# Later batches take the output slices in the order 3, 4, 1, 2, GpSimd casts part 1 of the weights, and ring loads stand two steps behind the stores

## What is computed

```python
masked_w = weight * mask[None, :, :]              # (8, 512, 512)
w_bot = jnp.einsum('bg,got->bot', y, masked_w)    # one 512x512 matrix for each of 128 batches
x = x + jnp.einsum('bnt,bot->bno', x, w_bot) + bias
```

## Time and profile before

| | us |
|---|---|
| median of three runs | 644.95 |
| lowest and highest of them | 641.86, 645.34 |
| the profiled execution, its own time | 650.79 |
| its span, first to last instruction | 649.0 |
| TensorE busy | 625.6 |
| ScalarE busy | 304.4 |
| VectorE busy | 306.9 |
| GpSimd busy | 109.0 |

### The profile page before, as it was taken

The page is one execution under the profiler, slowest core; times in us unless marked ns, Lnnn a source line. Parts: engine busy times, 40 slices in busy tenths (PEclk is TensorE's granted clock), DMA queues, the critical chain, the costliest instruction groups (busy, mean ns, idle before and its releaser), DMA issues.

```text
span 649.0 us, 18471 instructions
## 1 busy us (share of the span) xinstructions
PE 625.6 (96%) x7911; PEld 597.0 (92%) x7911; DVE 306.9 (47%) x328; ACT 304.4 (47%) x529; POOL 109.0 (17%) x92
## 2 busy tenths in 40 slices
PE   8999996979999978999999999999999999999997
PEld 3467996979999978999999999999999999999997
DVE  5996663758643432444343443434343443434221
ACT  0131673757755433554545544554545444554500
POOL 5796653566500000000000000000000000000000
PEclk9999997989999997999999999999999999999999
DMA  8999989998999995665789996665789997663112
GB/s 323 419 325 314 302 273 305 278 282 277 294 364 287 318 315 173 179 178 150 201 235 346 299 305 195 180 179 156 180 252 339 276 315 210 179 179 116 50 66 82
DMA packets 52400, 157.28 MB, mean 242 GB/s; under 512 B 7696, under 2 KB 20096, under 8 KB 40576
## 3 DMA queue, kind: packets, MB, share of 16 engines
q1 hardware_dynamic: 33200, 121.92, 62.3%
q10 hardware_dynamic: 19120, 34.19, 16.6%
HBM read 109.94 MB, written 46.14 MB: 240 GB/s over the span
## 4 chain that ended last, share of the span: by engine, by line
PE 86%; DMA 6%; DVE 4%; issue 2%; ACT 1%; POOL 1%; ACTq 0%; DVEq 0%
PE ps L584 66%; PE ps L565 15%; PE ps L544 5%; DMA xs<-in_x 4%; DVE raw L468 1%; DMA w_parts<-parts 1%; DVE wbot L481 1%; ACT wbot L423 1%; DVE ring L473 1%; DMA ring<-in_first 1%; POOL raw L382 1%; DVE staged L494 0%; POOL parts L384 0%; ACT parts L418 0%; ACT parts L414 0%
## 5 line engine op out<-in xcount | busy, mean ns | idle before, releaser
L584 PE MATMUL ps<-wbot,xs 128*128 128x128 f32 x4096 | 482.5, 278 | 6.9 <-DMA xs<-in_x 6.1
L584 PEld LDWEIGHTS ps<-wbot,xs 128*128 128x128 f32 x4096 | 469.8, 194 | 10.6 <-DMA xs<-in_x 6.5
L423 ACT ACTIVATE wbot<-ps 128x512 f32<-128x512 f32 x464 | 267.6, 611 | 238.8 <-PE ps L584 128.4
L494 DVE TENSOR_TENSOR staged<-ps,bias_sb 128x512 f32<-128x512 f32 x128 | 88.5, 691 | 310.1 <-PE ps L584 309.8
L473 DVE COPY ring<-ring 32x4096 bf16<-32x4096 bf16 x116 | 142.7, 1231 | 10.6 <-DMA ring<-w_parts 7.2
L565 PE MATMUL ps<-yv,ring 112*128 112x64 bf16 x3712 | 122.2, 193 | 11.3 <-ACT wbot L423 10.9
L565 PEld LDWEIGHTS ps<-yv,ring 112*128 112x128 bf16 x3712 | 119.3, 98 | 13.3 <-ACT wbot L423 12.4
L382 POOL TENSOR_TENSOR raw<-raw,parts 128x512 f32<-128x512 f32 x32 | 45.8, 1430 | 55.3 <-ACT parts L414 55.2
L468 DVE TENSOR_TENSOR raw<-raw,mask_sb 128x512 f32<-128x512 f32 x32 | 43.0, 1351 | 7.5 <-DMA raw<-in_w 7.0
L384 POOL TENSOR_TENSOR parts<-raw 128x512 bf16<-128x512 f32 x32 | 42.2, 1319 | 2.5
L414 ACT ACTIVATE parts<-raw 128x512 bf16<-128x512 f32 x32 | 20.0, 626 | 45.6 <-DVE raw L468 30.1
(11 more groups left out here) (13 smaller groups left out, 6.5 us busy)
## 6 DMA issues: line engine op xcount, KB each, us to landing
ring<-w_parts SPq DMA_DIRECT2D x232, 256.0 KB, 6.2
xs<-in_x SPq DMA_DIRECT2D x32, 1024.0 KB, 14.4
out<-staged ACTq DMA_DIRECT2D x128, 256.0 KB, 3.8
w_parts<-parts SPq DMA_DIRECT2D x32, 384.0 KB, 10.7
raw<-in_w SPq DMA_DIRECT2D x16, 512.0 KB, 11.3
mask_sb<-in_mask SPq DMA_DIRECT2D x8, 256.0 KB, 10.3
xs<-in_w SPq DMA_DIRECT2D x1, 1024.0 KB, 9.0
ring<-in_w SPq DMA_DIRECT2D x2, 512.0 KB, 16.6
```

Source lines behind the costliest of these rows:

```text
L423: eng.activation(chunk_place(b, k), chunk_sums(b, k), ACT.Copy).then_inc(s_ev_a, 1)
L494: eng.tensor_tensor(staged[:, n % OUTB, :].rearrange("p (b o) -> p b o", b=GB), ps2[n % S2B][:, :].rearrange("p (b o) -> p b o", b=GB), bi ...
L584: ins = eng.matmul(ps2[n % S2B][:, b * SL:(b + 1) * SL], xs[:, load % GROUPS * GB + b, k, :], at, start=(k == 0), stop=(k == KT - 1))
```

## The change

- Units 4 to 15 take the slices in the order 3, 4, 1, 2 (`slice_of`) instead of 1, 2, 3, 4; the host puts the output together accordingly. Units 4 and 5 so read parts that units 2 and 3 have read before, and the halves of tiles 20 to 31 are first used by units 6 and 7 (bursts 48 to 59). `fresh` and `tiles_of` follow.
- `TILES_AT` is written out. Tiles up to 19 keep their steps; 20 to 25 go to steps 15, 17, 18, 20, 21 and 23, and 26 to 31 to steps 35, 36, 37, 38, 40 and 41. Stores and raw loads follow by their rules.
- From step 5 on (`BY_POOL`) GpSimd casts part 1 in front of its two subtractions, and holds the wait for the store of tile t - 5. ScalarE keeps part 2.
- `kept` counts tiles stored two steps ago instead of one, so fresh ring loads stand a step later in SP's queue: bursts 20 to 22 in step 9 (8 before), 24 to 26 in 13 (12), 28 to 30 in 17 (16).

```diff
@@ -51,10 +51,9 @@
 
 
 EARLY = 4
-TILES_AT = {0: (4, 5)}
-for _t in range(EARLY + 2, TILES):
-    _n = 1 + (_t - EARLY - 2) * 15 // 16
-    TILES_AT[_n] = TILES_AT.get(_n, ()) + (_t,)
+TILES_AT = {0: (4, 5), 1: (6, 7), **{_t - 6: (_t,) for _t in range(8, 20)},
+            15: (20,), 17: (21,), 18: (22,), 20: (23,), 21: (24,), 23: (25,),
+            35: (26,), 36: (27,), 37: (28,), 38: (29,), 40: (30,), 41: (31,)}
 STORE_AT = {}
 for _n, _tiles in TILES_AT.items():
     _to = _n + (1 if _n < 5 else 2)
@@ -68,6 +67,8 @@
 RAW0 = 24
 WARM = 7
 
+BY_POOL = 5
+
 
 def bursts_before(n):
 
@@ -78,6 +79,11 @@
     return (n + GROUPS,) if n % GROUPS in (0, GROUPS - 1) else (n + GROUPS - 1, n + GROUPS)
 
 
+def slice_of(u):
+
+    return (u + (FU if u >= SLICES else 0)) % SLICES
+
+
 def x_load(n):
 
     u, gg = divmod(n, GROUPS)
@@ -103,13 +109,14 @@
 
 def fresh(b):
 
-    return b < FB + SLICES * CS
+    u, c = divmod(b, CS)
+    return b < SLICES * CS or u in (SLICES + FU, SLICES + FU + 1) and half_of(slice_of(u), c) >= FB // CH + 2
 
 
 def tiles_of(b):
 
     u, c = divmod(b, CS)
-    return (half_of(u % SLICES, c) + 1) * PER_HALF if fresh(b) else 0
+    return (half_of(slice_of(u), c) + 1) * PER_HALF if fresh(b) else 0
 
 
 def slot_of(b):
@@ -286,7 +293,7 @@
 
             def load_burst(b):
                 u, c = divmod(b, CS)
-                s, i = u % SLICES, slot_of(b)
+                s, i = slice_of(u), slot_of(b)
                 h = half_of(s, c)
                 if fresh(b):
                     for t in range(h * PER_HALF, (h + 1) * PER_HALF):
@@ -338,7 +345,7 @@
             loaded = FB
             kept = 0
             for n in range(1, STEPS):
-                kept = max((kept, EARLY if n >= 2 else 0, *(t + 1 for t in STORE_AT.get(n - 1, ()))))
+                kept = max((kept, EARLY if n >= 2 else 0, *(t + 1 for t in STORE_AT.get(n - 2, ()))))
                 for t in TILES_AT.get(n + RAW_AHEAD, ()):
                     if t > RAWN and t % 2 == 0:
                         load_raw(t)
@@ -376,6 +383,11 @@
             assert steps[0] == Y_STEPS
             spread_y(eng, 0).then_inc(s_yv, 1)
 
+            def cast_w1(t):
+                eng.wait_ge(s_mul, t + 1)
+                stored(eng, t - PARTN)
+                eng.tensor_copy(parts[:, t % PARTN, PART1, :], raw[:, t % RAWN, :]).then_inc(s_p1, 1)
+
             def subtract(t):
                 at, w1 = raw[:, t % RAWN, :], parts[:, t % PARTN, PART1, :]
                 eng.wait_ge(s_p1, t + 1)
@@ -403,6 +415,8 @@
                     if b < FB:
                         add_one(b)
                 for t in TILES_AT.get(n, ()):
+                    if n >= BY_POOL:
+                        cast_w1(t)
                     subtract(t)
 
         @block.scalar
@@ -451,8 +465,9 @@
                     store_out(n - 1)
                 for t in before:
                     cast_w2(t)
-                for t in TILES_AT.get(n, ()):
-                    cast_w1(t)
+                if n < BY_POOL:
+                    for t in TILES_AT.get(n, ()):
+                        cast_w1(t)
                 before = TILES_AT.get(n, ())
             store_out(STEPS - 1)
             for i in range(OUTB):
@@ -484,7 +499,7 @@
 
             def add_bias(n):
                 u, gg = divmod(n, GROUPS)
-                s = u % SLICES
+                s = slice_of(u)
                 if n == 0:
                     eng.wait_ge(s_bias, 16)
                     eng.wait_ge(s_y, Y_STEPS)
@@ -548,7 +563,7 @@
             def burst(b):
                 u = b // CS
                 turn, i = (b - FB) // RING, slot_of(b)
-                s, c = u % SLICES, b % CS
+                s, c = slice_of(u), b % CS
                 if b == FB:
                     eng.wait_ge(s_ones, 16)
                 if b == FB or b % W == 0:
@@ -672,6 +687,6 @@
 
     full = np.empty((NB, NN, NO), got.dtype)
     for u in range(UNITS):
-        s, first = u % SLICES, W * (u // SLICES)
+        s, first = slice_of(u), W * (u // SLICES)
         full[first:first + W, :, s * SL:(s + 1) * SL] = got[u].transpose(1, 0, 2)
     return full
```

## The result

| | before | changed |
|---|---|---|
| median | 644.51 us (4 runs, 641.86 to 645.34) | 626.0 us (4 runs, 625.24 to 626.83) |
| profiled execution, its own time | 650.79 us | 626.83 us |
| its span | 649.0 us | 625.0 us |
| TensorE busy | 625.6 us | 618.4 us |

The ratio is 0.972, with a 95% interval of 0.969 to 0.975: 2.8% faster. 626.0 lies inside the stated range of 625.5 to 638, at its low end; the forecast was 630.5. The profiled execution of the kernel before (650.79) is slower than all four timed ones, so the profiles are 24.0 us apart and the medians 18.5, where the forecast had 20.3 and 14.5.

What follows compares the result with a forecast made beforehand. TensorE's pace bounds the kernel; only three stalls and crumbs before 262 us, 24.3 us, can be won. Less 4.0 put back, net 20.3 takes the profiled 650.79 to 630.5 us; range 625.5 to 638.

Steps and rivals of the forecast that it cites:

- three stalls: TensorE idle at step 12, step 18 and steps 37 to 39: 7.6, 5.3 and 8.9 us with clock.
- the crumbs: TensorE's other seven waits for ScalarE's evictions, 2.5 us together; 1.0 counted as staying.
- the put-back of 4.0 us: Share of the 24.3 us won that was expected back: 2.0 + 0.5 + 0 + 1.0 + 0.5, net 20.3.
- A: Step 12: eviction behind ScalarE's cast waiting for tile 12's late store; 6.2 us idle, 1.4 clock, 7.6; 2.0 put back.
- B: Step 18: eviction delayed by step 16's two tiles; 3.7 us idle, 1.6 clock, 5.3; 0.5 left.
- C: Steps 37 to 39: x loads leave bunched after SP's waits; 6.1 us idle, 2.8 clock, 8.9; counted as gone.
- Late tiles: Traffic of six tiles moved late, at most 4.5 MB in steps 32 to 43: 0.5 us added, bounds 0 and 4.
- the 0.8 that I took: Assumed us for GpSimd's 128x512 cast of part 1, between 0.79 from below and 1.15 to 1.17 from above.
- a: Rival: a wait remains at the stores, their landing the real limit; 4 to 7 us more, 636; 15% with d's milder form.
- b: Rival: x stays late at steps 37 to 39, its loads saturating the queues; 638.5 us; 7%.
- c: Rival: GpSimd's waits for stores hold ScalarE's part 2 and TensorE as before; 643 us; 5%.
- d: Rival: GpSimd becomes the bound, one step's slack per row; 637 us at dearest prices, gain gone from 4.1 us a cast; slower 3%.

## Why the prediction was right, and where its terms were off

**What bounded the kernel** held: three stalls, their clock and the crumbs, 24.3 us. From profile to profile the time fell by 650.79 - 626.83 = 24.0. The split was a little off: the crumbs of 2.5 are waits of weight loads, of which TensorE's matmuls stood idle for only 1.2, at step 6; the rest shows in the busy time of the bursts. The step that failed is the put-back of 4.0 us: it measured 0.6, all of it the wait for x, which I had put at 0. That accounts for most of the distance between 630.5 and 626.0.

**A**, 2.0 put back, measured 0. The mechanism behind the term was there: the ring load of burst 20, issued at 91.33, reached VectorE by 96.72, after 5.4 us, where it had taken 3.2 (94.28 to 97.47) and the forecast feared 6.2. It cost VectorE 0.98 us (0.70 before) and TensorE nothing, because it left 3 us sooner than the forecast had it: the store of tile 11 left SP 1.2 us earlier and landed in 11.0 us instead of 12.7. For the same reason SP came to the store of tile 13 at 94.4, not 97.1, and the place of tile 18 was free. The forecast took 94.28 for fixed; the other profiles (extra casts aside) have it at 87.8 to 91.8, so the execution that it was read from was a late one, and that the term came out at nothing owes something to luck. That the wait at SP made A in the kernel before is read from its own trace, and the lag alone moves the store of tile 12 ahead as foreseen. But A is also missing from two profiles without lag and without GpSimd's cast (parted tiles alone; order and tile steps), so its absence in one profile proves little, and what the lag brings at A on the median is not measured. That GpSimd's cast would cure it too is half true: alone, it takes the wait off step 12 and hands a later one on to ScalarE's part 2.

**B**, 0.5 put back, measured 0. Its cause, two tiles in one step, is shown where the stores are in time: with the lag B stays at 3.57 (old steps) and goes with parted tiles; with order, cast and lag it stays at 3.81 under the old steps. With late stores, parting the tiles alone gains nothing.

**C** was counted as gone, and the wait was right within 0.6 us (a second profile of the changed kernel has no wait for x), but what I said of its landing was wrong. x loads were to land in 12 us or so, as in the next round. Issues of x in the changed kernel, and the last one alone (KB, us to landing):

```profile
160.73 0.62 SPq L320 DMA_DIRECT2D xs<-in_x  x1
165.29 3.05 SPq L320 DMA_DIRECT2D xs<-in_x  x2
174.48 0.42 SPq L320 DMA_DIRECT2D xs<-in_x  x1
183.36 0.43 SPq L320 DMA_DIRECT2D xs<-in_x  x1
187.96 0.44 SPq L320 DMA_DIRECT2D xs<-in_x  x1
192.53 0.42 SPq L320 DMA_DIRECT2D xs<-in_x  x1
201.78 0.43 SPq L320 DMA_DIRECT2D xs<-in_x  x1
...
xs<-in_x SPq DMA_DIRECT2D x1, 1024.0 KB, 22.3
```

They are spaced by steps, as foreseen, but the first lands in 6.6 us and the last in 22.3 (28.4 before), and TensorE needs it after 22: the margin is zero, hence the 0.6. In the kernel before, four loads leave between 196 and 204 us; with the lag alone at most two leave within 4 us of each other and no wait is left, though the last takes 20.9 us. The two other kernels with the old order and no lag wait 3.07 and 3.34 for x, and no kernel with the lag or the new order waits more than 1.25. So C was made by SP's waits bunching the loads, as the forecast said; the new slice order removes those waits too, but is not needed for it. Why the loads of this round land later than the next one's stays open; tile work's transfers just ahead of it are the obvious guess, untested.

**Crumbs**, 1.0 put back, measured 0: the casts of part 1 that stood before pairs were all of them, as the run without GpSimd's cast shows by bringing them back. **Late tiles**, 0.5 added, measured 0.

**GpSimd's cast**: 0.61 us, under the 0.8 that I took and under the lower bound of 0.79. The Trainium skill's price (GPSIMD Engine Reference, 3.1, 769 ns for 512 elements) is above it as well; the measurement decides. Made three times in a row the first two averaged 0.84.

**Rivals.** a and b did not occur. c is what GpSimd's cast does alone, at B. d's mechanism exists, but its formula took a tile's price and its slack both too favourably: the gain turns into a loss at about 2.9 us a cast, where the formula has 3.7 on the median. At the measured 0.61 the changed kernel stays clear of it.

## What to carry to other kernels

A DMA queue that waits in order for its own earlier stores delays everything behind it; put independent issues ahead of the wait before moving work between engines, because moving the work may only hand the wait on to the next engine in the chain. When several small stalls come from one late resource, one part alone can gain nothing and two together most: test parts both alone and left out. Slack of a helper engine is to be counted to the place where its result is read in order, not to the end of a step.

## What the runs showed of the hardware that I had not expected

Executions of the kernel before ran from 635.0 to 645.6 us in one group of thirteen and from 641.1 to 646.9 in another of eleven; the changed kernel's six ran from 625.2 to 627.2, and the four with a lag of three from 625.2 to 626.0. Stores that are asked for just as they land would make such a spread; that they do is a reading of the traces (A present at 94.3, absent at 90.0 and 89.0), not shown by a run of its own.

A 128x512 float32 to bfloat16 cast on GpSimd (0.61 us) is no slower than ScalarE's (0.63).
